# Reordering a step of a graph-attention pipeline: feed-forward chunks before exponentials, row scaling in two parts, edge mask and copy moved, x kept a step later

## The reference

```python
def gat(h, adj, W, a):
    Wh = h @ W
    e = Wh @ a[:128] + swap(Wh @ a[128:])         # one column plus one row, 512 x 512
    e = leaky_relu(e, 0.2)
    att = softmax(where(adj > 0, e, -9e15), axis=1)
    return att @ Wh
h = gat(x, adj, W1, a1)                           # round one
h = gat(h, adj, W2, a2)                           # round two
h = layernorm(x + h) * g_ln1 + b_ln1
h = layernorm(h + relu(h @ w_ff1 + b_ff1) @ w_ff2 + b_ff2) * g_ln2 + b_ln2
```

## Time and profile before

| | |
|---|---|
| median of 3 runs | 1142.9 us (1141.55 to 1143.61) |
| the profiled execution's own time | 1141.11 us |
| its span in the profile | 1139.3 us |
| granted TensorE clock, mean | 0.988 of full |
| busy: PE, DVE, ACT, POOL | 1037.4, 932.3, 705.4, 563.4 us |
| a full step of the first stage | 20.37 us, steps 3 to 15 |
| steps 0 to 2 end, the tail begins | 55.49 us, 320.54 us |

### The profile page before, as it was taken

How to read it: one execution, slowest core, us unless ns; L and a number is a source line. 1 busy time by engine, 2 the same in 40 slices (tenths; PEclk the granted TensorE clock), 3 DMA queues, 4 the chain that set the end, 5 groups by cost and what they waited for, 6 DMA issues and landing times. The chain is left out here.

```text
span 1139.3 us, 20494 instructions
## 1 busy us (share of the span) xinstructions
PE 1037.4 (91%) x5765; PEld 488.7 (43%) x5765; DVE 932.3 (82%) x2320; ACT 705.4 (62%) x1323; POOL 563.4 (49%) x506
## 2 busy tenths in 40 slices
PE   3588889888888799999999999999999999999997
PEld 3557667576664233333333333333333333244443
DVE  4898998989987778887888888888888888748787
ACT  2476777767765456665666666666666665654443
POOL 3112112121111388877887888888888887700000
PEclk9899999999999899999999999999999999999999
DMA  7131211312031313331433143223313330000001
GB/s 227 61 111 56 98 70 56 111 57 90 22 113 64 92 49 106 108 102 35 119 93 88 59 116 97 67 81 107 101 49 103 106 79 2 1 10 29 37 28 46
DMA packets 49279, 86.85 MB, mean 76 GB/s; under 512 B 8376, under 2 KB 35256, under 8 KB 44219
## 3 DMA queue, kind: packets, MB, share of 16 engines
q1 hardware_dynamic: 47018, 85.59, 24.6%
q10 hardware_dynamic: 2192, 0.47, 0.2%
HBM read 52.19 MB, written 29.36 MB: 72 GB/s over the span
## 5 line engine op out<-in xcount | busy, mean ns | idle before, releaser
L1597 DVE TENSOR_REDUCE top<-b_peak 128x1 f32<-128x512 f32 x488 | 320.3, 684 | 73.9 <-PE b_peak L1273 72.6
L1438 ACT ACTIVATE b_prob<-b_score 128x1024 f32<-128x1024 f32 x256 | 258.1, 1025 | 151.9 <-PE b_score L1288 106.2
L1787 POOL TENSOR_TENSOR b_picked<-b_prob,mask 128x512 f32<-128x512 f32 x192 | 234.2, 1240 | 58.1 <-ACT b_prob L1438 45.8
L1787 POOL TENSOR_TENSOR b_picked<-b_prob,b_mask 128x512 f32<-128x512 f32 x185 | 226.1, 1243 | 56.6 <-ACT b_prob L1438 46.1
L1064 POOL TENSOR_TENSOR a_hw_n<-a_hw,a_inv 128x512 f32<-128x512 f32 x16 | 16.7, 1043 | 221.7 <-issue 168.4
L804 ACT ACTIVATE a_att<-a_att,a_least 128x512 f32<-128x512 f32 x128 | 91.4, 715 | 32.4 <-DVE a_least L834 32.4
L1273 PE MATMUL b_peak<-b_k_stack,b_q_stack 96*128 96x512 bf16 x256 | 98.4, 384 | 6.6 <-DVE top L1597 6.2
L1273 PE MATMUL b_peak<-shared 96*128 96x512 bf16 x232 | 90.0, 389 | 7.5 <-DVE top L1597 4.0
L834 DVE CUSTOM_DVE_ANT_0 a_att<-a_att,a_no_edge 128x512 f32<-128x512 f32 x128 | 87.3, 700 | 0.0
L550 PE MATMUL a_mid<-a_h_t,wff 128*128 128x512 f32 x128 | 64.9, 626 | 14.4 <-ACT a_hid L798 12.8
L1288 PE MATMUL b_score<-shared 98*128 98x512 bf16 x256 | 77.3, 383 | 0.0
(11 more groups left out here) (230 smaller groups left out, 1891.9 us busy)
## 6 DMA issues: line engine op xcount, KB each, us to landing
a_adj_in<-in_adj SPq DMA_DIRECT2D x15, 1024.0 KB, 5.1
scratch<-shared SPq DMA_DIRECT2D x32, 384.0 KB, 3.0
shared<-scratch SPq DMA_DIRECT2D x16, 768.0 KB, 6.9
scratch<-shared SPq DMA_DIRECT2D x32, 256.0 KB, 2.1
b_q_stack<-scratch SPq DMA_DIRECT2D x8, 768.0 KB, 5.5
b_k_stack<-scratch SPq DMA_DIRECT2D x8, 768.0 KB, 8.2
a_x_t<-in_x_t SPq DMA_DIRECT2D x16, 256.0 KB, 2.6
xs<-in_x SPq DMA_DIRECT2D x16, 256.0 KB, 5.3
```

Of the source, the lines that this page charges most:

```text
L1438: act.activation(prob[s % 2][:, 2 * u:2 * u + 2, :], score[u][:, :, :], ACT.Exp, scale=float(DH) ** -0.5).then_inc(sem("exp_ready"), 1)
L1597: dve.tensor_reduce(top[g][:, hh, c:c + 1], peak[hh % 2][:, :], AX.X, ALU.max, negate=True).then_inc(sem("peak_read"), 1)
L1787: pool.tensor_tensor(picked[(NR * s + rel) % 2][:, hh, :], prob[s % 2][:, hh, :], m, ALU.mult).then_inc(sem("picked_pool"), 1)
```

## The change

- ACT, `step`: in a step with no round two (step 1), `lower(0)` goes ahead of the copies. `keep_x` moves from the end of step t to step t+1, behind `keep_h` (and once into the tail). Each `hidden` goes ahead of the exponentials: hidden 0, exps 0, hidden 1, exps 1, hidden 2, exps 2 and 3, hidden 3.
- DVE, `scores(0)`: `invert(1)` comes after the first mask and not the second; `add_h` after the second mask and not after the last `leak`.
- DVE, `scale_rows`: takes its own reciprocals, for three chunks once three exponentials are there, then for the fourth; it comes directly after `scores(0)`, with `norm_stats(1)` behind it. `inv_ready[0]` counts two per graph.
- DVE, rest of the step: `norm_mean(1)` directly after `norm_stats(1)`, then `edges`, `norm_shift`, `add_x`; `keep_hw` ahead of `first_shift`.

```diff
--- before.py
+++ after.py
@@ -669,8 +669,12 @@
             def step(t, par, begin, first, second, feed, more):
                 if second:
                     lower(1, t - 2)
+                elif first:
+                    lower(0, t - 1)
                 if feed:
                     keep_h(t - 3)
+                    if t >= 4:
+                        keep_x(t - 4)
                 if begin:
                     act.wait_ge(row_ready[0], t)
                     act.wait_ge(xw_done, t + 1)
@@ -678,13 +682,13 @@
                     act.copy(s1_own[:, :, :].rearrange("p (a c) o -> p a c o", a=2),
                              both.rearrange("p a (c d) -> p a c d", c=2)[:, :, :, D + 3:D + 4]).then_inc(s1_ready, 1)
                     act.copy(xw[:, t, :, :].rearrange("p (a c) d -> p a (c d)", a=2), both).then_inc(xw_ready, 1)
-                if first:
+                if second:
                     lower(0, t - 1)
-                for chunks, chunk in (((0,), 0), ((), 1), ((1,), 2), ((2, 3), 3)):
+                for chunk, chunks in enumerate(((0,), (1,), (2, 3), ())):
+                    if feed:
+                        hidden(t - 3, chunk)
                     if second:
                         exps(1, t - 2, chunks)
-                    if feed:
-                        hidden(t - 3, chunk)
                 if first:
                     exps(0, t - 1, range(C))
                 if begin:
@@ -697,14 +701,13 @@
                 if second:
                     rstds(0, t - 2)
                     finish(t - 2)
-                if feed:
-                    keep_x(t - 3)
 
             def tail():
 
                 lower(1, B - 2)
                 lower(0, B - 1)
                 keep_h(B - 3)
+                keep_x(B - 4)
                 act.wait_ge(scaled[0], B - 1)
                 first_qk.first_part(act, pair[:, 0, :], 0, 0)
                 first_qk.first_part(act, pair[:, 1, :], 0, 1)
@@ -798,7 +801,7 @@
                 act.activation(hid[:, f, :], mid[f % 2][:, :], ACT.Relu, bias=w["bff1"][0][:, f:f + 1]).then_inc(hid_ready, 1)
 
             def exps(k, b, chunks):
-                act.wait_ge(inv_ready[k], b)
+                act.wait_ge(inv_ready[k], (2 - k) * b)
                 for c in chunks:
                     act.wait_ge(masked[k], C * b + c + 1)
                     act.activation(att[k][:, c, :], att[k][:, c, :], ACT.Exp, bias=least[k][:, c:c + 1], scale=-1.0,
@@ -850,11 +853,11 @@
                 for c in chunks:
                     if c + 1 < C:
                         leak(k, b, c + 1, s2)
-                    if c == 2:
+                    mask(k, b, par, c)
+                    if c == 0:
+                        invert_other()
+                    if c == 1:
                         add()
-                    mask(k, b, par, c)
-                    if c == 1:
-                        invert_other()
 
             def invert(k, b):
                 dve.wait_ge(scaled[k], b)
@@ -895,10 +898,15 @@
                 last.then_inc(rest_normed, 1)
 
             def scale_rows(b):
+
                 dve.wait_ge(hw_done, b)
-                dve.wait_ge(inv_ready[0], b + 1)
-                for c in range(C):
-                    last = dve.tensor_scalar(xw_n[:, c, :], xw[:, b, c, 0:D + 2], inv[0][:, c:c + 1], None, ALU.mult)
+                for n, chunks in enumerate((range(C - 1), range(C - 1, C))):
+                    at = slice(chunks[0], chunks[-1] + 1)
+                    dve.wait_ge(exp_ready[0], C * b + chunks[-1] + 1)
+                    dve.reciprocal(inv[0][:, at], total[0][:, at]).then_inc(inv_ready[0], 1)
+                    dve.wait_ge(inv_ready[0], 2 * b + n + 1)
+                    for c in chunks:
+                        last = dve.tensor_scalar(xw_n[:, c, :], xw[:, b, c, 0:D + 2], inv[0][:, c:c + 1], None, ALU.mult)
                 last.then_inc(scaled[0], 1)
 
             def keep_hw(b):
@@ -935,31 +943,27 @@
                 if first:
                     scores(0, t - 1, 1 - par, s2_own, range(C), (lambda: invert(1, t - 2)) if second else (lambda: None),
                            (lambda: add_h(t - 3)) if feed else (lambda: None))
+                if first:
+                    scale_rows(t - 1)
                 if feed:
                     norm_stats(1, t - 3)
-                if first:
-                    invert(0, t - 1)
-                    scale_rows(t - 1)
+                    norm_mean(1, t - 3)
                 if isinstance(t, int) and t == 1:
                     prep.vector_late(dve)
-                if feed:
-                    norm_mean(1, t - 3)
-                if second:
-                    add_x(t - 2)
+                if begin and t != 1:
+                    edges(t, par)
                 if feed:
                     norm_shift(t - 3)
                 if second:
+                    add_x(t - 2)
                     norm_stats(0, t - 2)
                     norm_mean(0, t - 2)
-                if begin and t != 1:
-                    edges(t, par)
-                if second:
-                    first_shift(t - 2)
                 if first:
                     keep_hw(t - 1)
                 if begin and t == 1:
                     edges(t, par)
                 if second:
+                    first_shift(t - 2)
                     finish_rest(t - 2)
                 if begin:
                     see(t)
@@ -977,7 +981,6 @@
                 first_qk.remainder(dve, pair[:, 1, :], 0, 1)
                 scores(0, B - 1, 1, s2_own, range(C // 2, C))
                 add_h(B - 3)
-                invert(0, B - 1)
                 scale_rows(B - 1)
                 norm_stats(1, B - 3)
                 norm_mean(1, B - 3)
```

## The result

The changed kernel takes 1147.49 us (median of 4 runs, 1147.29 to 1147.85) against 1142.88 before: ratio of the runs 1.0044, 95% interval 1.0031 to 1.0057, so **slower by 0.4%**; by the medians it is 4.6 us. The profiled execution took 1147.39 us with a span of 1145.6; against the profiled execution of before (1141.11, span 1139.3) that is +6.3. The profiled execution of before lay 1.8 under its median, and the runs of that kernel spread from 1140.5 to 1144.2 over the whole study. The traces therefore carry a sum of +6.3, the medians one of +4.6.

What follows compares the result with a forecast made beforehand. DVE was taken to bound the step, with PE close behind. Terms 15.7 - 0.4 - 6.6 - 0.2 gave +8.5 us, a median of 1151.4 (0.7% slower); forecast's own range 1146.5 to 1155, 8-in-10 range 1141.5 to 1156.5.

Steps and rivals of the forecast that it cites:

- The scores' end: DVE, full step from its first leak: add_h waits for the feed-forward sum, so scores end at 11.81, not 11.00: +0.81 us.
- The second exponential, not the last hidden, is what the new order puts in front of feed_up: ACT and PE: claim about what precedes feed_up, with the feed-forward sum hardly moved, 9.27 us against 9.12 before.
- the fixed 9.3: Feed-forward sum ready 9.27 us after the step's first leak, hardly moved, while DVE comes for it at 8.38 and waits.
- The rival that the sum would no longer be late: At add_h: the sum is ready at 8.4 when DVE comes, so the kernel is faster, 1136.1 to 1139.6 us; chance 0.13.
- Scaling: DVE, two-part scaling with statistics behind, up to norm_mean(1): 2.92 us against 2.22, its waits now uncovered: +0.70.
- the 0.29 of four columns: DVE: 0.29 us taken for a reciprocal with its wait ahead of a scaling, used for both parts of the scaling.
- Edges to norm_mean(0): DVE, norm_mean(1) to norm_mean(0): edges and norm_shift held by POOL's encode, add_x loses its wait; 4.00 us against 3.38: +0.62.
- The end: DVE, norm_mean(0) to next step: edges gone, only keep_hw covers the first norm's latency; 2.85 us against 3.77: -0.92.
- +1.21: Sum of the four terms for a full step: +1.21 us, making a step of 21.6.
- Steps 0 to 2: Start: first leak at 12.5 us (-4.1), keep_hw earlier, step 2's wait for round two shrinks (-1.3); together -6.6, bounds -4.1 and -7.
- The tail: Tail: reciprocal of three chunks free while the last exponential runs, -0.2 us; keep_x on ACT +0.5 at most; taken as -0.2.
- +8.5: Total forecast change in us: 15.7 for full steps, -0.4 for step 3, -6.6 for the start, -0.2 for the tail.

Runs made afterwards that it cites:

- run 2: Changed kernel with invert(1) and add_h back in their old places between the chunks of scores(0): 1140.12 us, ratio 0.9983 to the kernel before.
- run 5: Changed kernel with only invert(1) back behind the second mask, add_h staying ahead of the last leak: 1148.80 us, ratio 1.0061 to the kernel before.
- run 6: As run 5, with hidden 0 and hidden 1 back to back on ACT and later hiddens one exponential's group earlier: 1142.62 us, ratio 1.0006.
- run 3: Changed kernel with norm_stats(1) back ahead of scale_rows, which keeps its two parts: 1136.67 us, ratio 0.9952 to the kernel before.
- run 9: Changed kernel with POOL's encode of a full step waiting until norm_shift is done: 1140.58 us, ratio 0.9983 to the kernel before.
- run 1: Kernel before with one edit: in step 1 lower(0) goes ahead of the copies on ACT: 1137.76 us, ratio 0.9960.
- run 11: Kernel before with only the scaling in two parts, each with its own reciprocal, norm_stats(1) still ahead: 1137.81 us, ratio 0.9957.
- run 7: Changed kernel with invert(1) behind the second mask, hiddens early on ACT, and norm_stats(1) ahead of scale_rows: 1132.24 us, ratio 0.9913 to the kernel before.
- run 8: Changed kernel with keep_x back at the end of ACT's step, behind finish: 1151.42 us, ratio 1.0077 to the kernel before.

## Why the prediction was right, and where its sizes were off

**The sign and the mechanism** were right. Taken one by one, in a step:

- *The scores' end, forecast +0.81, measured +0.91.* The feed-forward sum was the wait (runs 2, 5, 6). "The second exponential, not the last hidden, is what the new order puts in front of feed_up" should have named the exponential between the hiddens; the effect and the fixed 9.3 were right. The rival that the sum would no longer be late is refuted: DVE came at 9.28 behind a held mask and, with the mask free (run 5), stood idle for 0.92. Run 6 shows that this exponential is 0.41 of that wait.
- *Scaling, forecast +0.70, measured +0.55* (14.68 - 11.91 against 13.22 - 11.00). Of the waits 0.34 and 0.25 are idle as named; a reciprocal with its wait ahead of the scaling costs 0.19 to 0.21 on three columns or one, and I took the 0.29 of four columns; why that one is longer no run shows. Run 3 gives back 0.79 by the order alone.
- *Edges to norm_mean(0), forecast +0.62, measured +0.44* (3.82 against 3.38). edges was held for 0.07 and not 0.17. norm_shift was held for 0.4 as before, but I had entered the length of its record, 0.58, where its slot is 0.48 (0.51 before). I had put both holds together at 0.7 to 0.8; run 9 shows that without them the step is 0.46 shorter. The Trainium skill (SBUF — State Buffer, "Who interferes with whom") has it that a VectorE and a GpSimd instruction which both need the ports that the two engines share shut each other out, each for a whole instruction. This case's rows bear it out both ways, by norm_shift's 0.56 against 0.15 on DVE and the encode's 3.54 against 2.69 on POOL.
- *The end, forecast -0.92, measured -0.93.* keep_hw covers the root but for 0.18, first_shift starts 1.14 after the mean, the leak 2.84 after it.

Sum of a step +0.97 where +1.21 stood: 12.3 over the thirteen steps instead of 15.3, and 0.7 of the 12.3 is the one late step, which the forecast did not have. **The term of the forecast that was sized wrong furthest is this one**, through the two middle terms.

*Steps 0 to 2, forecast -6.6, measured -5.3.* The first leak came at 12.44 as worked out (-4.1). Two later gains came out smaller. Step 1 took 17.00 and not 17.74 (-0.7 for -1.2): graph 1's encode, begun at about the same time (16.64 for 15.82), now fell upon the last mask and the scalings. And step 2 took 20.73 and not 21.18 (-0.45 for -1.3), for the reason below.

*The tail, forecast -0.2, measured -0.7.* The reciprocal was ready at once behind add_h (0.16 with no idle, where 0.29 of idle stood before). How much of the 0.7 is this is not settled: run 1, whose tail is that of the kernel before, took 68.3 for it where before took 67.6.

The terms of the trace give -2.2 against my +8.5; the other 1.7 between +6.3 and the medians' +4.6 is spread between executions, mostly of the kernel before. So the time moved by a little over half of what was forecast and lies near the low end of the forecast's own range, 1146.5 to 1155. The misses partly cancel: 3.0 too much in the full steps against 1.3 too much gain at the start.

## What to carry to other kernels

In a list that one engine works off in order, a wait costs its idle only where nothing else is at hand: two groups of instructions that each have a gap should stand crosswise so that each fills the other's (run 3), and a consumer should be called where its input is ready, not where it would be nice to have it (runs 2 and 5). Before moving a consumer forward, find the producer's own bound; here one exponential on another engine was 0.4 of a wait of 0.9 (run 6). And a change of many moves should be timed move by move: this one holds two edits that gain 3 to 5 us each when they stand alone (runs 1 and 11), and its other moves give that back in the full steps. Three small edits to it (run 7) make it 1.3% faster.

## What the runs showed of the hardware

**A short instruction pays for a long neighbour.** norm_shift works on 128x4 and takes 0.15 alone (run 9), and 0.36, 0.56 or 0.58 beside the encode. Which of these it is depends on how far POOL's chunk has come when DVE asks, for its record ends with that chunk: at 234.23 where the chunk ends at 234.21 (before; the chunk starts at 233.60), at 232.25 for 232.23 (run 11), at 237.88 for 237.87 (changed kernel). In the last of these the chunk itself had been held by edges, and it went ahead of norm_shift.

**A hold costs what isn't hidden.** The mask held for 0.53 by POOL's scaling costs nothing in the changed kernel, where the feed-forward sum is later still (run 5), and 0.37 in run 8, where the sum is ready sooner.

**The clock in step 2.** Round two of graph 0 is 32 matmuls that come after 8.5 to 9.8 us in which PE stood idle. Timeline of PE, changed kernel and then the kernel of run 7:

```profile
37.97 6.18 PE L567 MATMUL a_turn<-a_hw_n,a_att 128*128 128x128 f32 x32 [8.52 <-POOL a_hw_n L1067]
```

```profile
39.25 6.57 PE L567 MATMUL a_turn<-a_hw_n,a_att 128*128 128x128 f32 x32 [9.79 <-POOL a_hw_n L1067]
```

Before, the same 32 matmuls took 5.35 us from 44.12; in a full step they take 3.74 at a granted clock of 1.00. The granted clock over them was 0.69 of full before, 0.59 in the changed kernel and 0.55 in run 7: at the lower of its two levels, 1.2 of 2.4 GHz, for a longer part. Step 2 waits for them, so an earlier start does not carry through whole. I had priced them at their length of before. The length of the idle alone doesn't settle how long they take: it is 9.79 in the kernel before, in run 1 and in run 7, and they took 5.35, 6.03 and 6.57. What else does is open.
